# Message passing over sorted edges: ready-made words per step in four layers and three convolutions

## The reference

```python
edge_index = jnp.stack([src, dst])
h = jnp.maximum(_layernorm(x), 0.0)
x = x + _L0_gnn_ref(h, src, dst, ...)      # attention: softmax over the edges of each target
h = jnp.maximum(_layernorm(x), 0.0)
x = x + _L1_gnn_ref(h, edge_attr_16, ...)  # 4 layers: segment_sum(relu(x[src] + ea), dst), two products, norm
h = jnp.maximum(_layernorm(x), 0.0)
x = x + _L2_gnn_ref(h, edge_index, ...)    # 2 convolutions: segment_sum(h[row] * norm, col) and a product
h = jnp.maximum(_layernorm(x), 0.0)
x = x + _L3_gnn_ref(h, edge_index, ...)    # 1 convolution: segment_sum(x[src] @ W, tgt) + x @ W_self
```

## Time and profile before

| | |
|---|---|
| median of three runs | 8802.96 us |
| span of the profiled execution | 10778.7 us |
| PE busy | 5733.6 us (53%) |
| POOL busy | 6208.7 us (58%) |
| DVE busy | 3226.3 us (30%) |
| ACT busy | 1207.5 us (11%) |
| mean granted TensorE clock | 0.726 of full speed |

### The profile page before, as it was taken

How to read it: one execution, slowest core, us unless ns; L and a number is a source line. 1 busy time by engine, 2 the same in 40 slices (tenths; PEclk the granted TensorE clock), 3 DMA queues, 4 the chain that set the end, 5 groups by cost and what they waited for, 6 DMA issues and landing times.

```text
span 10778.7 us, 140823 instructions
## 1 busy us (share of the span) xinstructions
PE 5733.6 (53%) x23750; PEld 3992.8 (37%) x23751; DVE 3226.3 (30%) x7228; ACT 1207.5 (11%) x2511; POOL 6208.7 (58%) x6737
## 2 busy tenths in 40 slices
PE   4566547566675666656665566653344334333344
PEld 2333336334443334433343333332333223332334
DVE  3444564212231123312232123331222122321222
ACT  1111026311111111101111111110000000000000
POOL 4555535566555655466554655546666666656665
PEclk7666669788887888878887788775666555665666
DMA  6777644333332333233332333221111111111111
GB/s 182 217 218 216 200 131 117 88 87 84 85 82 80 88 82 85 75 85 87 84 85 72 89 82 85 74 52 46 46 48 48 44 47 46 47 41 45 46 48 46
DMA packets 948126, 946.53 MB, mean 88 GB/s; under 512 B 414507, under 2 KB 681958, under 8 KB 947556
## 3 DMA queue, kind: packets, MB, share of 16 engines
q0 software_dynamic: 213248, 462.82, 16.1%
q1 hardware_dynamic: 626384, 393.18, 13.6%
q10 hardware_dynamic: 108436, 89.99, 2.6%
HBM read 799.72 MB, written 152.12 MB: 88 GB/s over the span
## 4 chain that ended last, share of the span: by engine, by line
another core or an unknown queue 45%; PE 21%; issue 16%; DVE 7%; DVEq 6%; DMA 2%; ACTq 1%; ACT 1%; POOL 1%; SPq 0%; POOLq 0%
PE ps_seg L944 9%; PE ps_big L1024 8%; DVE onehots L1542 2%; DVEq L1542 1%; PE ps_mm L911 1%; DMA rows<-value_rows_by_edge 1%; PE ps_big L900 1%; DVEq L396 1%; PE ps_t L968 1%; DVEq L1565 1%; PE ps_big L944 1%; DVE gate L1718 0%; ACT onehots L1246 0%; DVE h_res L1722 0%
## 5 line engine op out<-in xcount | busy, mean ns | idle before, releaser
L794 POOL DMA_INDIRECT rows<-node_rows,idx x5488 | 5203.2, 948 | 3579.6 <-SPq L660 1611.1
L944 PE MATMUL ps_seg<-rows,onehots 128*128 x6864 | 1408.4, 375 | 2294.2 <-DVE onehots L1542 1669.7
L1565 DVE TENSOR_TENSOR sums<-sums,ps_seg 128x128 f32 (+1 forms) x1830 | 525.0, 287 | 5862.7 <-remote 3715.4
L944 PE MATMUL ps_seg<-onehots 128*128 128x128 f32 x7840 | 1272.7, 314 | 1713.9 <-DVE onehots L1542 810.3
L944 PEld LDWEIGHTS ps_seg<-rows,onehots 128*128 128x128 f32 x6864 | 1245.4, 274 | 2450.2 <-issue 2444.6
L944 PEld LDWEIGHTS ps_seg<-onehots 128*128 128x128 f32 x7840 | 1201.4, 225 | 2348.7 <-ACT onehots L1246 1287.7
L1542 DVE SCALAR_TENSOR_TENSOR onehots<-ps_mm,win_base,dst_ch 128x512 f32<-128x512 f32 x1845 | 1384.0, 750 | 561.1 <-issue 495.2
L1024 PE MATMUL ps_big<-q_res,ident 128*128 (+1 forms) x1960 | 1207.5, 703 | 129.6 <-issue 76.3
L1024 PE MATMUL ps_big<-rows,ident 128*128 (+1 forms) x1960 | 1107.1, 649 | 0.0
L1246 ACT ACTIVATE onehots<-ps_big 128x512 f32<-128x512 f32 x980 | 571.8, 597 | 4310.2 <-remote 2157.3
L794 POOL DMA_INDIRECT sums<-kv_rows,idx x784 | 741.2, 945 | 538.7 <-SPq L658 274.2
(11 more groups left out here) (205 smaller groups left out, 2532.6 us busy)
## 6 DMA issues: line engine op xcount, KB each, us to landing
q_res<-gates_by_edge SPq DMA_DIRECT2D x784, 256.0 KB
rows<-node_rows,idx POOLq DMA_INDIRECT x5488
rows<-dst_padded SPq DMA_DIRECT2D x196, 256.0 KB
value_rows_by_edge<-sums SPq DMA_DIRECT2D x196, 256.0 KB
gates_by_edge<-gate ACTq DMA_DIRECT2D x196, 256.0 KB
rows<-value_rows_by_edge SPq DMA_DIRECT2D x196, 256.0 KB, 3.2
node_rows<-h_res ACTq DMA_DIRECT2D x49, 448.0 KB
sums<-kv_rows,idx POOLq DMA_INDIRECT x784
```

Source lines behind the costliest of these rows:

```text
L794: pool.indirect_dma_start(target[:, r, j, :], None, table, bass.IndirectOffsetOnAxis(ap=idx[:, half, r, j:j + 1], axis=0)).then_inc(rows_l ...
L944: last = nc.tensor.matmul(banks[u % len(banks)][:, 0:width], onehots[:, u, j, :], rhs(j), start=j == 0, stop=j == J - 1)
L1565: V.tensor_tensor(mine, mine, seg_banks(k)[(u - 1) % len(seg_banks(k))][:, 0:width], ALU.add).then_inc(agg_added, 1)
```

## The change

A second form of the step table is made beside the packed one. Five fields per step (window offset in `sums`, slot offset in the ring, chunk count, end of group, ended group) are stored as words and brought back by eleven small loads, arranged by turns of four steps (`sum_words` of eight words a turn for DVE, `row_words` of twelve for PE and ACT). The positions of the edges relative to the window of each step are made once: POOL fetches the `dst` rows of all steps with two indirect DMAs, DVE subtracts the window's base, SP stores them (512 KB) and loads them back as `away`, four words per partition and step. Both lie in `q_res`, behind the slots for gates. In layers and convolutions each engine works out semaphore values and addresses for four steps ahead of the waits, DVE makes a one-hot matrix from `away` without table fields, the wait for rows moves from DVE to PE in the convolutions, and ACT no longer waits for `segsum_ready`. The attention passes keep their loops. `load_weights` first calls the new `load_words`.

```diff
+            def load_words():
+                sp.wait_ge(away_made, 2)
+                sp.dma_start(away_d.rearrange("(g p) e -> p g e", p=P), away_rows[:, :, :]).then_inc(away_stored, 16)
+                sp.wait_ge(words_stored, 16)
...
+                    (sum_words[0:1, :, 0:4], by_turn(SUM_, BEFORE, 4)),
...
+                    (row_words[0:1, :, 11:12], by_turn(ENDED_, 0, 1)),
+                ):
+                    sp.dma_start(to, source).then_inc(words_loaded, 16)
+                sp.wait_ge(away_stored, 16)
+                sp.dma_start(away.rearrange("p (s j) -> p s j", j=J),
+                             away_d[BEFORE:BEFORE + LAST + 2, :].rearrange("s (p j) -> p s j", j=J)).then_inc(away_loaded, 16)
+
             def load_weights():
+                load_words()
                 sp.dma_start(score[:, RING:CHUNKS, :], by_chunk(weight_d)[:, RING:CHUNKS, :]).then_inc(weights_loaded, 16)
...
+            for g in range(2):
+                pool.indirect_dma_start(away_rows[:, g, :], None, dst_d.rearrange("(c e) -> c e", e=CHUNK),
+                                        bass.IndirectOffsetOnAxis(ap=chunk_of[:, g:g + 1], axis=0)).then_inc(away_fetched, 16)
...
-                def edge_layer(s, u, turn, row):
-                    if not (isinstance(s, int) and s == LAST):
-                        add_gates(s + 1, row.get(CHUNK_, CHUNKS - 1, 1), row.get(SLOT_, RING - 1, 1), 1 - u)
-                    sum_segments(k, s, u, row, D, lambda j: msg[:, u, j, 0:D], (msg_ready,), (l * N_STEP + s + 1,))
+                    told = [pe.compute_val(i * UNROLL + add_base + (n + 1)) for n in range(1, UNROLL + 1)]
+                    marked = [pe.compute_val(i * UNROLL + mark_base + n) for n in range(1, UNROLL + 1)]
...
+                            pe.wait_ge(rows_ready, landed[n - 1])
+                            add_gates(up_to(words[n], (RING - 1) * CHUNK), 1 - u, marked[n - 1])
...
+                        sum_messages(u, told[n - 1])
...
-                    wait_alone(act, "act", segsum_ready, s + (l + 1) * N_STEP - (0 if is_first(s) else 1))
-                    act.wait_ge(gates_added, l * N_STEP + s + 1)
+                    act.wait_ge(gates_added, added)
...
-            def mark_next(k, s, u, row):
-                if isinstance(k, int):
-                    dve.wait_ge(rows_ready, row.get(CHUNK_, CHUNKS - 1, 1) + (sum_no(k) * CHUNKS + 1))
-                mark_edges(k, s + 1, 1 - u, row.get(CHUNK_, CHUNKS - 1, 1), row.get(WIN_, WINDOWS, 1))
+            def mark_step(at, u):
+                V.scalar_tensor_tensor(onehots[:, u, :, :],
+                                       numbers.rearrange("p (a n) -> p a n", a=1).to_broadcast([P, J, P]), 0.0,
+                                       away[:, ds(at, J)].rearrange("p (j a) -> p j a", a=1).to_broadcast([P, J, P]),
+                                       ALU.add, ALU.is_equal).then_inc(onehot_ready, 1)
...
+                    upto = [dve.compute_val(i * UNROLL + base + n) for n in range(UNROLL + 1)]
+                    for n in range(1, UNROLL + 1):
+                        mine = sums[:, ds(up_to(words[n - 1], (WINDOWS - 1) * AGGW), D)]
+                        at = i * (UNROLL * J) + (n + 1) * J
+                        dve.wait_ge(agg_added, upto[n - 1])
+                        dve.lower_ap(mine)
+                        dve.lower_ap(away[:, ds(at, J)])
+                        dve.wait_ge(segsum_ready, upto[n])
+                        V.tensor_tensor(mine, mine, ps_seg[(n - 1) % 2][:, 0:D], ALU.add).then_inc(agg_added, 1)
+                        mark_step(at, (n + 1) % 2)
```

More of the change, by code:

```diff
@@ L1 @@
-from contextlib import ExitStack
+from contextlib import ExitStack, contextmanager
 import itertools
@@ L57, in build_program @@
     N_STEP = LAST + 1
-    N_AGG = LAST
+    N_AGG = LAST + 1
     ctx = ExitStack()
@@ L425, in engine_loop, with each_turn, make_turn, clamped @@
             return eng.Fori(first, end)
+        def each_turn(eng, name, table, columns, body, turns=(0, LAST // UNROLL)):
+            def make_turn(i):
+                regs = [eng.alloc_register(f"{name}_word{n}_{next(load_no)}") for n in range(columns.stop - columns.start)]
+                eng.load(regs, table[0:1, ds(i, 1), columns].rearrange("a i n -> a (i n)"))
+                body(i, [eng.snap(r, donate=True) for r in regs])
+                for r in regs:
+                    eng.free_register(r)
+            begin, end = turns
+            if end - begin == 1:
+                make_turn(begin)
+            else:
+                with engine_loop(eng, begin, end) as i:
+                    make_turn(i)
+        @contextmanager
+        def clamped(eng, words, least, most):
+            regs = [eng.alloc_register(f"clamped{n}_{next(load_no)}") for n in range(len(words))]
+            for r, value in zip(regs, words):
+                eng.reg_alu(r, value, least, ALU.max)
+            yield [up_to(eng.snap(r, donate=True), most) for r in regs]
+            for r in regs:
+                eng.free_register(r)
+        def up_to(value, most):
+            return nc.s_assert_within(value, 0, most, skip_runtime_bounds_check_because="the table holds no more")
         def each_window(eng, body):
@@ L996, in _, with chunk_words @@
             attend_sum(GROUPS - 1)
+            pe.wait_ge(words_loaded, 16 * WORD_LOADS)
+            def chunk_words(tile_, slot, first, count):
+                return tile_.rearrange("p s j d -> p (s j d)")[:, ds(slot + first, count)]
             with pe.Fori(0, LAYERS) as l:
@@ L1016, in layer_sum, with add_gates @@
                                  lambda h: wait_alone(pe, "pe", node_h_ready, (l * GROUPS + g) * 2 + (h + 1)))
[L1018 to L1022, removed]
+                add_base = pe.snap(l * N_STEP)
+                def add_gates(slot, u, marked):
+                    for source in (gates, ring):
+                        pe.lower_ap(chunk_words(source, slot, 0, CHUNK))
@@ L1037, in _ @@
+                for begin, end, more in ((0, TURNS_ - 1, True), (TURNS_ - 1, TURNS_, False)):
+                    each_turn(pe, "pe", row_words, slice(0, 12), lambda i, words: layer_steps(i, words, more), (begin, end))
                 for part in (layer_turn, layer_hidden, layer_sum):
@@ L1535, in _ @@
             add_skip(EARLY, GROUPS)
+            dve.wait_ge(away_fetched, 32)
+            for g in range(2):
+                V.tensor_scalar(away_rows[:, g, :], away_rows[:, g, :], base_of[:, g:g + 1], None, ALU.subtract)\
+                    .then_inc(away_made, 1)
             chain(V.tensor_copy(numbers, iota_f[:, :]))
```

202 lines of the change are left out of this document (150 added, 52 removed).

## The result

The changed kernel takes 8830.56 us (median of 8 runs, 8821.88 to 8836.68), the kernel before 8804.83 us (8 runs). The ratio is 1.0029, with 95% interval 1.0019 to 1.0040: slower by 0.3%, a small but clear loss, beyond the 8821 us from which the prediction called it slower, and 13.6 us above the predicted 8817. One of the 8 runs of the kernel before took 10424.53 us; without it its median is 8802.96, the difference 27.6 us instead of 25.7 and the ratio 1.0031. A later set of runs gave 1.0023 (1.0013 to 1.0032).

What follows compares the result with a forecast made beforehand. The prediction took POOL's gathers (6272 at 1.25 us, 7840 us) to bound the kernel. Its terms 27.6 + 1.5 - 7 - 4 - 3.6 = +14.5 us on 8803 gave 8817 us, range 8570 to 8860.

Steps and rivals of the forecast that it cites:

- The bound: Whole kernel: POOL's 6272 gathers at 1.25 us each, 7840 us, set the time, with about 960 us outside them; chance 0.62.
- without a recording PE's signals come in time: PE's late signals to DVE (8.26 us) belong to the recording alone, so POOL hardly waits in unprofiled runs.
- The loads ahead of the weights: SP's queue in pass 1: store, eleven loads and `away` delay the weights by 27.6 us, 20.6 of it `away`.
- POOL's wait before the eighth chunk: Sign in the pass over values: this wait grows from 14 to about 40 us.
- The beginning: Seven more small operations while the table is made: +1.5 us (0 to 4).
- Pass ends and rows: Register work saved at seven pass ends, -7 us; convolutions' wait for rows moved to PE, -3.6 us at three ends.
- The last groups of a layer: POOL waits for slots there too; 1 us saved in each of four layers, -4 us.
- The middle of a pass: Layers and convolutions: register work, estimated at 0.5 us a step over both engines, lies under the gathers; nothing taken.
- a matrix at 0.75 us: Sign in the profile after: DVE's line for the one-hot matrix stays at 0.75 us.
- The steps still bound part of the time: Rival, chance 0.28, faster: gathers take 1.15 us without a recording, so saved step work shows; 8531 or 8731 us.
- The dear small pieces: Rival, chance 0.07, slower: `away`'s pieces in SP's queue before the weights cost 74 us instead of 20.6; 8870 us.
- Register work not saved: Rival, chance 0.03: clamping and addresses worked out again keep the register work, losing savings of 11 us; 8828 us.

Runs made afterwards that it cites:

- experiment 5: The kernel before with only the first of a chunk's four gathers issued in layers and convolutions: 6254.56 us.
- experiment 1: The kernel before, unedited, run again for a profile in the condition of the medians: 8800.94 us, span 8799.1.
- experiment 2: The changed kernel with the eleven loads of words and the load of `away` moved behind the second pass: 8807.39 us, ratio 1.0003 to the kernel before.
- Experiment 4: The kernel of experiment 2 with the store of the words moved from the beginning to behind the store of the distances: 8812.13 us, ratio 1.0008.
- experiment 6: The kernel of experiment 4 with only the first of a chunk's four gathers issued in layers and convolutions: 6029.80 us.
- experiment 12: The kernel of experiment 5 with the convolutions' wait for rows moved from VectorE to TensorE: 6633.56 us, with late signals in pass 0.
- experiment 3: The changed kernel with the load of `away` alone moved behind the second pass: 8814.92 us, ratio 1.0011 to the kernel before.
- experiment 9: The changed kernel, unedited, again beside the kernel before: 8829.31 us against 8808.00, ratio 1.0023.
- experiment 7: The kernel of experiment 6 with six dead operations a step on VectorE ahead of the addition, which did not reach the chip: 6334.44 us, signals late.
- experiment 8: The kernel of experiment 6 with six dead operations on TensorE ahead of the wait for rows, which did not reach the chip: 6336.20 us, signals late.
- experiment 10: The kernel of experiment 6 with six dead operations a step on VectorE between addition and matrix, which did not reach the chip: 6031.47 us.
- experiment 11: The kernel of experiment 6 again, without dead operations: 6034.15 us.

## Why the prediction was right, and where its steps were not

The range of 290 us would have held a saving of 230 us as well, and the three directions had 0.32, 0.34 and 0.34. That the time fell inside says little; what can be judged are the terms.

**The bound (right, from a wrong reason).** "A gather costs POOL 1.25 us even when nothing holds it": 1.249 us in both kernels, and experiment 5 shows that they were the bound. Taking POOL's waits off the disturbed span (8893) pointed to the right kernel, and the 1043 us outside the gathers, which did not fit 960, are 940 in experiment 1. But the prediction went on that "without a recording PE's signals come in time". The profiles of experiment 1 and of the changed kernel are recordings without a "remote" wait, and unrecorded runs of the kernel before took 10783 and 10792 us. By the rule of the Trainium skill (NOTIFIC — the notification-queue block, section 7.1) that I leaned on, the lateness would have belonged to the recording alone; the measurements decide against that use of it. What makes the signals late is open.

**The loads ahead of the weights (right).** Predicted 27.6, measured 27.6 in the whole stretch, and experiment 2 takes 19.6 of it away by moving the loads. That the two agree to the tenth is luck: with the other profiles of the same code the growth is 22 to 28 us, and its parts came out otherwise: `away` 16.5 instead of 20.6 (it lands after 20.5, as predicted, but costs 4 us less than that), the words 3.1, and 8.0 for store and gathers, where the prediction had 7.0 for all thirteen issues and nothing for the gathers (the last two near the scatter). POOL's wait before the eighth chunk grew from 14 to 39 us, as said (about 40).

**The beginning (the term that was mis-sized).** "Seven small operations more while the table is made ... +1.5 (0 to 4)". It was +7.5. The step costed the arithmetic and left out the DMA that goes with it: the store of the words, passed on SyncE's queue ahead of the clearing of the table and of the stores of keys. The prediction had priced small pieces at one place of that queue and not at the other. Experiment 4 shows it.

**Pass ends and rows (right in sum, one cause not borne out).** Predicted -7 and -3.6; the six gaps and the tail gave -3.1, -4.6 and -4.0, together -11.7. That these are savings of the workers fits experiments 5 and 6 (the gaps and the tail are shorter there too: the last 32.9 before, 25.5 after). But the -3.6 was given to the rows' wait on TensorE, and experiment 12, which moves that wait alone, has the three ends of the convolutions at 33.2, 40.7 and 33.6 us where experiment 5 has 30.1, 40.3 and 32.9: it shortens none. In experiment 6 they are 25.7, 32.5 and 25.5, so the saving there comes with the rest of the change.

**The last groups of a layer (wrong sign).** Predicted -4; the layers' gathers grew by 5.9 us. In four other profiles of kernels with the change (experiments 2, 3, 4 and 9) the four layers sum to 3939 to 3942 against 3932.9 in the only undisturbed profile before; 3.8 of the 5.9 us are the fourth layer's. With few gathers the sign is the same: 2852.7 to 2856.3 in five profiles with the change (6, 7, 8, 10 and 11), 2843.7 and 2849.5 in two with the layers of the kernel before (5 and 12). The size is near the scatter, and the cause is open.

**The middle of a pass (right).** "I take nothing": convolutions +0.5 in all. It is cover, and experiment 6 gives its size when the cover is gone, 0.30 us a step in the convolutions and nothing in the layers, where the prediction's estimate was 0.5 over both. The register work itself did go, 0.46 us a step in a convolution and 0.71 in a layer over all engines in experiment 6. The sign that the prediction named, a matrix at 0.75 us, did not come: it takes 0.68.

**The rivals.** "The steps still bound part of the time" fell: its mechanism is real and worth 225 us, but its condition (a gather of 1.15 us) was not met. The dear small pieces fell (20.5 us, not 74). "Register work not saved" fell by the count, 113604 instructions against 140823.

In sum: forecast +14.5, found +25.7 by the medians and +33.0 by the profiles; of the 18.5 between forecast and profiles 6.0 are the beginning, 9.9 the layers' gathers, 3.2 the scatter of pass 0, and the rest small terms of both signs. What was mis-sized is the beginning, by a store that the sum left out; the layers' term had the wrong sign.

## What to carry to other kernels

Before pricing a cut in register work, find what sets the pace of the step: here 27000 fewer instructions were worth nothing in 7840 us of gathers, and 225 us once these were thinned out, 218 of them in the convolutions. Price the data that a table of ready values needs as transfers in a queue, at every place where they stand: here 5 KB in pieces of 4 bytes took 12.1 us and 492 KB in pieces of 16 bytes 20.5, and what waits is the large transfer behind them. Before dead work is used to double a cost, look in the trace whether it is there.

## What was not expected of the hardware

5 KB in 4-byte pieces (1280 of them) took 12.1 us to land and made a 3136 KB transfer behind them land 8.3 us later (10.4 to 18.7; 17.5 in experiments 2, 3 and 9). That is 9 ns a piece, where 31488 pieces of 16 bytes took 20.5 us, 0.65 ns a piece. Signals from TensorE to other engines can be late in whole sets of runs, recorded or not: VectorE's addition then waits 7.4 us on average for them, 500 times, and the same kernel takes 10783 us instead of 8805. With a quarter of the layers' and convolutions' gathers no such wait was left in those passes, while pass 0, with all of its gathers, kept them; softmax and values, which have no gathers for rows, show a single one of 0.6 us in all profiles. So the lateness, when it comes, stands in the stretches with dense gathers; more was not found.
